# A graph kernel on one core: out-degree adjacency built and transposed in bfloat16, eight weight transposes placed elsewhere, last output tile in halves

## What is computed

```python
def _L2_gnn_ref(x, edge_index, weight, bias):          # "GCN"
    support = x @ weight
    adj = jnp.zeros((n, n), dtype=x.dtype).at[edge_index[0], edge_index[1]].set(1.0)
    adj = adj + jnp.eye(n, dtype=x.dtype)
    degree = adj.sum(axis=1, keepdims=True)
    d_inv_sqrt = jnp.where(degree > 0, jax.lax.rsqrt(degree), 0.0)
    adj_normalized = d_inv_sqrt * adj * d_inv_sqrt.T
    out = adj_normalized @ support + bias
...
    def _sage_conv(x, src, dst, Wl, bl, Wr, num_nodes):  # block four, two layers of it
        agg = jax.ops.segment_sum(x[src], dst, num_segments=num_nodes)
        cnt = jax.ops.segment_sum(jnp.ones((src.shape[0],), x.dtype), dst, num_segments=num_nodes)
        agg = agg / jnp.maximum(cnt, 1.0)[:, None]
        return agg @ Wl.T + bl + x @ Wr.T
...
    x = x + _L0_gnn_ref(relu(layernorm(x)), ...)         # symmetric adjacency, three hops
    x = x + _L1_gnn_ref(relu(layernorm(x)), ...)         # four relations, then an FFN
    x = x + _L2_gnn_ref(relu(layernorm(x)), ...)
    x = x + _L3_gnn_ref(relu(layernorm(x)), ...)
```

## Time and profile before

| what | value |
|---|---|
| median of 3 runs | 353.31 us (353.21 to 353.43) |
| the profiled execution's own time | 353.74 us |
| its span, first to last instruction | 351.9 us |
| PE busy | 342.6 us, 97% of the span |
| DVE busy | 238.7 us, 68% |
| POOL, ACT busy | 141.1 us, 87.4 us |

### The profile page before, as it was taken

How to read it: one execution, slowest core, us unless ns; L and a number is a source line. 1 busy time by engine, 2 the same in 40 slices (tenths; PEclk the granted TensorE clock), 3 DMA queues, 4 the chain that set the end, 5 groups by cost and what they waited for, 6 DMA issues and landing times.

```text
span 351.9 us, 4344 instructions
## 1 busy us (share of the span) xinstructions
PE 342.6 (97%) x1617; PEld 242.3 (69%) x1617; DVE 238.7 (68%) x404; ACT 87.4 (25%) x188; POOL 141.1 (40%) x117
## 2 busy tenths in 40 slices
PE   8999999997999999999999999999999998999996
PEld 3459888784478888888888888844474543474454
DVE  4899999998698887970595615426664569653543
ACT  3465664323300000000001042213462331112110
POOL 5000000006599999999402020551125340672120
PEclk9999999999999999999999999999999999999999
DMA  7100003359600000060300199930000000000003
GB/s 227 71 1 4 3 2 118 123 146 292 220 0 2 0 1 2 0 239 0 91 0 2 53 282 188 185 129 0 0 0 2 2 0 0 2 0 0 2 0 121
DMA packets 18486, 22.07 MB, mean 63 GB/s; under 512 B 2016, under 2 KB 10720, under 8 KB 18464
## 3 DMA queue, kind: packets, MB, share of 16 engines
q1 hardware_dynamic: 17936, 20.85, 21.9%
q0 software_dynamic: 240, 0.79, 0.8%
q10 hardware_dynamic: 288, 0.13, 0.1%
HBM read 20.72 MB, written 1.05 MB: 62 GB/s over the span
## 4 chain that ended last, share of the span: by engine, by line
PE 86%; DVE 10%; ACT 2%; DMA 1%; issue 1%; ACTq 0%; DVEq 0%
PE bank L1621 14%; PE bank L1564 14%; PE bank L1731 13%; PE bank L1507 12%; PE bank L1687 8%; PE bank L604 4%; PE bank L1771 4%; PE bank L577 4%; PE bank L1719 4%; PE bank L601 3%; DVE h L1204 2%; PE bank L593 2%; PE bank L1494 2%; DVE lo L1222 1%; DMA bias<-in_edge_type 1%; DVE wall L1376 1%
## 5 line engine op out<-in xcount | busy, mean ns | idle before, releaser
L888 POOL TENSOR_TENSOR spare<-slots 128x512 f32<-128x512 f32 x4 | 6.0, 1494 | 76.5 <-PE bank L1507 75.8
L1013 ACT ACTIVATE columns<-mean_var,eps 128x1 f32<-128x1 f32 x16 | 4.7, 293 | 118.7 <-DVE mean_var L1153 118.7
L1621 PE MATMUL bank<-slots,wall 128*128 128x256 f32 x128 | 30.2, 380 | 0.0
L1507 PE MATMUL bank<-h_t,spare 128*128 128x256 f32 x128 | 28.1, 379 | 0.0
L1687 PE MATMUL bank<-slots 128*128 128x512 f32 x64 | 28.0, 592 | 0.0
L604 PE MATMUL bank<-slots 128*128 128x112 bf16 x256 | 27.8, 228 | 0.0
L1621 PEld LDWEIGHTS bank<-slots,wall 128*128 128x128 f32 x128 | 24.2, 190 | 3.2
L1507 PEld LDWEIGHTS bank<-h_t,spare 128*128 128x128 f32 x128 | 24.2, 190 | 3.2
L601 PE MATMUL bank<-slots 128*128 128x140 bf16 x128 | 26.2, 242 | 0.0
L387 DVE TENSOR_TENSOR slots<-slots 128x1792 bf16<-128x1792 bf16 (+1 forms) x27 | 25.0, 984 | 0.0
L1376 DVE STREAM_TRANSPOSE wall<-slots 128x512 f32<-128x512 f32 x16 | 16.4, 1077 | 12.1 <-DMA slots<-in_L_gnn_Wl 10.6
(11 more groups left out here) (262 smaller groups left out, 758.7 us busy)
## 6 DMA issues: line engine op xcount, KB each, us to landing
slots<-in_L_gnn_W_rel SPq DMA_DIRECT2D x4, 1024.0 KB, 10.4
spare<-in_L_gnn_W_ffn SPq DMA_DIRECT2D x1, 2048.0 KB, 8.0
slots<-in_L_gnn_W_ffn SPq DMA_DIRECT2D x1, 2048.0 KB, 8.8
slots<-in_L_gnn_Wl SPq DMA_DIRECT2D x8, 256.0 KB, 9.9
slots<-in_L_gnn_Wr SPq DMA_DIRECT2D x8, 256.0 KB, 8.7
x<-in_x SPq DMA_DIRECT2D x4, 256.0 KB, 6.1
bias<-in_L_gnn_W SPq DMA_DIRECT2D x2, 512.0 KB, 5.9
slots<-in_L_gnn_W_self SPq DMA_DIRECT2D x1, 1024.0 KB, 5.5
```

Source lines behind the costliest of these rows:

```text
L1507: ins = pe.matmul(bank, left, right, start=start and i == 0, stop=stop and i == len(pairs) - 1)
L1621: ins = pe.matmul(into, left[:, k, tile(p)], right[:, k, :], start=(n in (0, 2, 3, 5) and r == 0 and k == 0), stop=False, skip_group_check ...
```

## The change

- `out_degrees` writes (count > 0) + identity as bfloat16 into `linked` (the whole of `both_ways` seen as bfloat16, four tiles) and sums it in the same instruction: four instructions for nine.
- `transpose_counts` multiplies `linked` by a bfloat16 identity in place of the float32 transpose; what lands in PSUM is already the adjacency with self-loops. PE gets a wait on `deg_ready` ahead of it.
- `adjacency(t)` is one ACT copy; `with_own` on POOL is gone.
- A scratch row (`agg_step`) moves from `both_ways` to `h_t`.
- The eight `turn` calls: two follow each of the down tiles 0, 1 and 2 on DVE (2,0 to 2,3, then 3,0 and 3,1), and the last two (3,2 and 3,3) come after the pair `p = 0` of sage layer one.
- The last tile's mean of layer two is made in two halves of 256 columns in two banks, finished by two DVE instructions, and stored by two DMAs, one of SP and one of ACT.

```diff
-        agg_row, agg_step = b0[:], both_ways[:, 0, 0:HALF]
+        agg_row, agg_step = b0[:], h_t[:, 0, HALF:N]
+        linked = both_ways[:].rearrange("p a n -> p (a n)").bitcast(BF16).rearrange("p (t n) -> p t n", t=NT)
+        ident_b = eye[:, N - P:N]
...
-            for m in range(NT):
+            for m in range(NT - 1):
                 sp.wait_ge(sage_out[1], m + 1)
                 sp.dma_start(out[m * P:(m + 1) * P, :], x[:, m, :]).then_inc(out_stored, 16)
-            sp.wait_ge(out_stored, 16 * NT)
+            sp.wait_ge(sage_out[1], NT)
+            sp.dma_start(out[N - P:N, side[0]], x[:, NT - 1, side[0]]).then_inc(out_stored, 16)
+            sp.wait_ge(out_stored, 16 * (NT + 1))
...
-            def with_own(t):
-                own = adj[:, t, t * P:(t + 1) * P]
-                pool.wait_ge(steps_out, 2 * t + 2)
-                pool.tensor_tensor(own, own.bitcast(F32), ident[:], ALU.add).then_inc(adj_ready, 1)
...
                 act.wait_ge(cnt_t_ready, t + 1)
-                act.activation(both_ways[:, t % 2, :], (misc_bank if t % 2 else cnt_bank)[:], ACT.Relu, bias=ones[:, 0:1], scale=-1.0)\
-                    .then_inc(steps_out, 1)
-                act.wait_ge(steps_out, 2 * t + 1)
-                act.activation(adj[:, t, :], both_ways[:, t % 2, :], ACT.Relu, bias=ones[:, 0:1], scale=-1.0).then_inc(steps_out, 1)
+                act.activation(adj[:, t, :], (misc_bank if t % 2 else cnt_bank)[:], ACT.Copy).then_inc(adj_ready, 1)
...
+            act.wait_ge(sage_out[1], NT + 1)
+            act.dma_start(out[N - P:N, side[1]], x[:, NT - 1, side[1]]).then_inc(out_stored, 16)
...
                 for t in range(NT):
-                    link(dve.tensor_scalar(both_ways[:, t % 2, :], count[t], 0.0, None, ALU.is_gt))
-                    link(dve.tensor_reduce(out_deg[:, t:t + 1], both_ways[:, t % 2, :], AX.X, ALU.add))
-                link(dve.tensor_scalar(out_deg[:], out_deg[:], 1.0, None, ALU.add))
+                    ins = dve.scalar_tensor_tensor(linked[:, t, :], count[t], 0.0, eye_of(t), ALU.is_gt, ALU.add, accum_out=out_deg[:, t:t + 1])
+                link(ins)
                 dve.tensor_scalar(eps_deg[:], out_deg[:], EPS, None, ALU.mult).then_inc(deg_ready, 1)
...
                 if m < NT - 1:
+                    for k in range(2):
+                        turn(2 + m // 2, 2 * (m % 2) + k)
                     continue
...
-                        if layer == 0:
-                            for k in range(2, KT):
-                                turn(3, k)
...
-                    if (layer, p) == (0, 0):
-                        for k in range(KT):
-                            turn(2, k)
...
                     if (layer, p) == (0, 0):
-                        for k in range(2):
+                        for k in range(2, KT):
                             turn(3, k)
...
+                    if (layer, m) == (1, NT - 1):
+                        for i, bank in enumerate((main[m], psum[4])):
+                            dve.wait_ge(mean_ready[1], m + i + 1)
+                            dve.scalar_tensor_tensor(x[:, m, side[i]], bank[:, side[i]], inv_in[:, m:m + 1], x[:, m, side[i]],
+                                                     ALU.mult, ALU.add).then_inc(sage_out[1], 1)
+                        continue
...
-                        ins = pe.transpose(bank[:, tile(s)], count[s][:, tile(t)], ident[:])
+                        ins = pe.matmul(bank[:, tile(s)], linked[:, s, tile(t)], ident_b, start=True, stop=True)
...
                     if (m, g) in ((1, 7), (2, 0)):
+                        pe.wait_ge(deg_ready, 1)
                         transpose_counts(range(m - 1, m))
...
+                    if (layer, m) == (1, NT - 1):
+                        mean(layer, m, exact, main[m], side[0])
+                        mean(layer, m, exact, psum[4], side[1])
+                    else:
+                        mean(layer, m, exact, main[m], slice(0, N))
```

More of the change, by code:

```diff
@@ L815, in run_blocks @@
         up_ready, up_out, down_ready, down_out = sem("up_ready"), sem("up_out"), sem("down_ready"), sem("down_out")
-        steps_out, gcn_hi, last_lo, gcn_lo, near_ready, even_near_out, odd_near_out, gcn_ready, gcn_out = (
-            sem("steps_out"), sem("gcn_hi"), sem("last_lo"), sem("gcn_lo"), sem("near_ready"), sem("even_near_out"), sem("odd_near_out"), sem("gcn_ready"), sem("gcn_out"))
+        gcn_hi, last_lo, gcn_lo, near_ready, even_near_out, odd_near_out, gcn_ready, gcn_out = (
+            sem("gcn_hi"), sem("last_lo"), sem("gcn_lo"), sem("near_ready"), sem("even_near_out"), sem("odd_near_out"), sem("gcn_ready"), sem("gcn_out"))
         wide_t_ready, sage_s_ready = sem("wide_t_ready"), sem("sage_s_ready")
@@ L987, in split_scaled @@
                 pool.tensor_tensor(lo[1][:, t, :], h[:, t, :], hi[1][:, t, :].bitcast(F32), ALU.subtract).then_inc(gcn_lo, 1)
-            for t in range(2):
+            for t in range(NT - 1):
                 split_scaled(t)
[L991 to L994, removed]
             pool.wait_ge(last_lo, 1)
@@ L1762, in sage_products, with mean @@
                         fill_h(*between[n])
-            def mean(layer, m, exact):
+            def mean(layer, m, exact, into, columns):
                 for q in range(NT):
@@ L1769, in mean @@
                     for part in (hi[layer], lo[layer]):
-                        left, right = (cnt_r, part[:, q, :]) if exact else (wall[:, R], part[:, q, :].bitcast(F32))
-                        ins = pe.matmul(main[m][:], left[:, q, tile(m)], right, start=(q == 0 and part is hi[layer]),
+                        left, right = (cnt_r, part[:, q, columns]) if exact else (wall[:, R], part[:, q, columns].bitcast(F32))
+                        ins = pe.matmul(into[:, columns], left[:, q, tile(m)], right, start=(q == 0 and part is hi[layer]),
                                         stop=(q == NT - 1 and part is lo[layer]))
@@ L1779, in means @@
                         pe.wait_ge(own_sum, 4 * layer + 2)
-                    mean(layer, m, exact)
+                    if (layer, m) == (1, NT - 1):
[3 more added lines that the diff above has]
+                        mean(layer, m, exact, main[m], slice(0, N))
                     if layer == 0 and m >= 2:
```

## The result

| | before | changed |
|---|---|---|
| median of 22 runs each | 353.37 us | 352.53 us |
| ratio | | 0.9977, 95% interval 0.997 to 0.9983 |
| profiled execution: own time, span | 353.74, 351.9 | 352.38, 350.5 |

The forecast was 352.55 us, 0.2% less; measured is 0.84 us or 0.23% less. The two profiled spans differ by more, 1.4 us.

A forecast was written before the change was run, and what follows sets the result against it. PE's work and its few waits, two through DVE and one at the end, were taken to bound the kernel. +1.36 - 1.64 - 0.48 = -0.76 us gave 352.55 us; own range 352.1 to 353.6, eight in ten 351.4 to 354.3.

The forecast's parts named there:

- DVE becomes the pace: Down stage: two turns (2.0 us) behind each tile exceed DVE's idle; period 7.65 us, `hi` of tile 3 +1.36 us.
- The forecast waits of PE: In `near`: about 1.2 us before column block 3, then about 1.6 us for `hi` of tile 3, inside the 1.36.
- P3: Product on PE in sage layer one, held by DVE's L1467; with turns taken out, it starts without a gap: -1.64 us.
- Out-degrees: Four DVE instructions for nine, ahead of a 3.70 us DVE wait for PE: value 0.
- Transposes: Sixteen on PE, bfloat16 at 0.06 us each against 0.11: value 0, at most 0.8 us if PE set the pace.
- rival A: Moved turns hidden in DVE's down-stage idle, PE keeps the pace: -2.5 us, 350.8 us; chance 0.08.
- The end: Last tile of layer two in halves: PE passes +0.16, last DVE step -0.27, store -0.37; together -0.48 us.
- The PE term: Last tile's mean: sixteen 256-column passes at about 0.125 us, 2.0 against 1.84: +0.16 us; bounds +0.0 and +1.7.
- The store: Last store of the kernel: half the bytes behind the last DVE step, -0.37 us; bounds 0 and -0.4.
- Rival B: Down stage: DVE slowed beside POOL, 0.9 us for each of three tiles: +1.9 us, 355.2 us; chance 0.08.
- C: Rival in sage layer one: something else holds P3, its 1.64 us do not come back: +0.88, 354.2 us; chance 0.07.
- D: Rival in `near`: PE's clock falls to 1.2 GHz after two waits, eight passes take twice as long: 354.7 us; chance 0.05.

## Why the prediction was right

*Overall.* The parts are forecast as they came out, but that -0.76 lies so near to the -0.83 of the traces is in part luck: at the end two terms are off by -0.18 (PE) and +0.15 (the store), and they cancel.

*DVE becomes the pace.* Right, in size too: steps of 7.68, 7.72 and 7.63 us between the adds against 7.65, a pair of turns 2.03 (239.98 to 242.01) against 2.0, and +1.39 against +1.36. The run with three turns a tile shows that it is the pace and not a coincidence. The forecast waits of PE, 1.2 and 1.6 us, are 0.88 and 1.56, each from start to start less one step of 0.23 (0.72 and 1.40 in the idle columns). So the first was put too long; it is no term of the sum, since both end with DVE's chain. The statement that the chain of before started at DVE's add was not quite so: it came through ACT's adjacency passes, and those are the 0.05 that the prediction allows for ACT.

*P3.* Right to 0.01 us. DVE's L1457 ran at 291.08, 0.20 behind the start of P4, where 0.14 was worked out.

*Out-degrees.* DVE's wait behind them grew from 3.70 to 5.48 us, and nothing waited for them, as worked out.

*Transposes.* 0.055 us each against 0.06. Alone they give 0.32 us. In the changed kernel, where DVE sets the pace, next to nothing is left, as the sum had it: `hi` of tile 3 comes 28.63 us after the first down chain, and 28.73 with the old transposes. The rival A (350.8), in which PE keeps the pace and everything else is won, did not happen. But it describes the version with the turns ahead of the down stage, at 350.64.

*The end.* Right in sum, -0.51 against -0.48, with two terms off the other way from each other. The PE term was mis-sized: 0.125 us a pass was expected, 0.113 measured, so sixteen halves take the time of eight wholes. No row of before had 256 columns in f32r, and the fixed part of 0.017 that I took from 512 columns does not show there. The store gave 0.22 (0.25 in the run with the halves alone), not 0.37: from issue to the span's end are 2.36 us before, 2.14 here, and 2.36 with one store. In slices of 0.05 us the bytes of the last store move for 0.80 us before (350.35 to 351.15) and for 0.50 here (349.20 to 349.70). So half the bytes took 0.30 less and not half of the time, and the rest of the way grew by 0.08. The size of the store and its queue are not told apart: the 128 KB of SP's queue took 1.9 us to land and those of ACT's 1.7, and no run stores the last half from SP. The Trainium skill, "DMA: Bandwidth & Descriptors", section on the anatomy of one DMA, would give 0.30 us by its 436 GB/s; the time in which bytes move shrank by as much (0.30), while the way to the landing as a whole shrank by 0.22.

*Rival B,* DVE slowed beside POOL, did not happen at the adds (0.65 to 0.70), though the mechanism exists. The row that gave its price, L1437, reads two operands from SBUF, while the adds read one from PSUM; the last section shows what that makes. *C* did not happen: P3 has no idle. *D* did not happen in the changed kernel: the granted clock stays 1.00 there. The upper end of the prediction's own range uses 1.5 for P3 and 0.1 for the end, and it gives no working for these two.

## What to carry to other kernels

Work moved off one stall is free only where the idle of its engine, per step of the loop, is larger than the piece: compare the two numbers row by row (2.0 against 1.25 to 1.75 here) before placing it, and count the period, since a deficit adds up over the steps. A gain of another engine in the same stage is worth next to nothing once that deficit exists (0.10 of 0.37 us here), so parts of a change that each look good may give less together. And look for the one long idle stretch first (11 us here): a delay at the head of a stage with slack is absorbed, a delay in each step is not.

## What the runs showed of the hardware

**Behind a wait of 2.65 us PE's clock fell in the profiled execution; behind waits of 0.72, 1.40 and 1.49 it did not.** In the run with three turns a tile PE idled for 2.65 us before block 3 of `near`. Its windows (stretch, length, busy times of PE, PEld, DVE, ACT, POOL, granted clock, DMA):

```profile
260.00:262.00 2.00, 1.87 (x5) 1.52 (x6) 1.47 (x5) 0.78 (x2) 0.36 (x1) 0.61 0.00 0
262.00:264.00 2.00, 2.00 (x6) 1.52 (x6) 1.90 (x4) 0.00 (x0) 0.00 (x0) 0.53 0.00 0
264.00:266.00 2.00, 2.00 (x11) 1.42 (x9) 1.10 (x5) 1.20 (x2) 0.00 (x0) 1.00 0.00 0
```

and four of its PE rows: the first behind the wait, one before and one after the clock came back, and the one that needs `hi` of tile 3:

```profile
260.13 0.55 PE L1500 MATMUL bank<-adj,hi 128*128 128x512 f32 x1 [2.65 <-DVE h L1379]
...
262.18 0.63 PE L1500 MATMUL bank<-adj,lo 128*128 128x512 f32 x1
...
264.35 0.40 PE L1500 MATMUL bank<-adj,lo 128*128 128x512 f32 x1
...
266.00 1.17 PE L1500 MATMUL bank<-adj,hi 128*128 128x512 f32 x4
```

The passes stepped by 0.43 us at the lower level of 1.2 GHz and by 0.23 at 2.4 GHz. It cost no time: the slower passes filled the wait for `hi` of tile 3. ACT had written that by 265.86, and PE went on at 266.00, 0.14 later, as in the changed kernel. The other executions of this run say the same. Of its ten, five have a mean granted clock of 0.995, which is what such a dip makes (3.4 us at half rate in 352.5), and five have 1.000; both groups begin at 354.3 us. So the same kernel keeps its clock in half of its executions, and the length of the wait alone doesn't decide it (that PE waited as long in them is inferred, since they have no trace). The Trainium skill, "TensorE: Matmul & The Clock Gate", section on HAM oscillation, warns that a wait in which PE idles long brings the half rate; the profiled execution agrees in kind.

**Half a microsecond lies in the first microseconds.** The same four products stand among the first rows of PE in the trace of before:

```profile
5.90 1.65 PE L536 MATMUL bank<-both_ways 128*128 128x512 bf16 x4
```

and in that of the changed kernel:

```profile
5.58 1.03 PE L536 MATMUL bank<-both_ways 128*128 128x512 bf16 x4
```

They took 1.65 us in the one and 1.03 in the other, where the steps had already halved, and the first product of the projection (L577) began at 9.7 and at 9.2. The windows view gives the granted clock as 1.00 there in both, so what halves the steps is not seen in it. The profiled runs of the other versions, with the same code up to there, have it between 9.2 and 9.8. So two single profiles of this kernel can differ by half a microsecond before any changed code runs, which is why the table above measures from the first down chain.

**DVE beside POOL.** In the changed kernel one instruction of the aggregation that used to take 0.75 took 1.84 us:

```profile
184.72 1.84 DVE L1345 SCALAR_TENSOR_TENSOR h<-h_t,inv_degs,h 128x512 f32<-128x512 f32 x1
184.75 1.26 POOL L978 TENSOR_TENSOR h<-h,bias 128x512 f32<-128x512 f32 x1 [13.98 <-PE bank L1490]
```

The shorter out-degrees had moved it to the very moment of a POOL addition. It lay ahead of a DVE idle of 5.48 us and cost nothing. Which rows feel POOL can be read from the whole timeline of the changed kernel, from 60 us on. Take DVE's single rows of two tensors of 128x512 (TENSOR_TENSOR and SCALAR_TENSOR_TENSOR) that overlap a POOL row by over 0.1 us. The 46 with an operand in PSUM (`bank`) took 0.65 to 0.75 us, as without POOL. The 28 with all operands in SBUF took 0.71 to 1.84, 27 of them 0.86 or more, where without POOL they take 0.68 to 0.75. No run changed the operands alone, so this is an observation. Turns took 1.03 to 1.16 us in all these traces, beside POOL too, so they hardly feel it. With all turns ahead of the down stage, tile 1's chain met POOL (L1162, two operands in SBUF, 0.99 us for 0.75) and took 6.11 us (241.67 to 247.78) in place of 5.65; DVE's idle took it up.
